# A vision tower on one core: patch loads issued by two engines in turn, and two bias products moved

## The reference

```
h = _L0_tok_ref(x, L0_tok_W, L0_tok_b)            # patches (576 x 768) @ W.T + b
h = _layernorm(h + _L0_attn_ref(h, ...))          # begins with a layer norm of h, then
                                                  # u, v, base = silu(xn @ W + b), v's bias is L0_attn_bv
```

## Time and profile before

| what | us |
|---|---|
| median of 3 executions | 157.12 |
| the three | 157.12, 155.45, 157.18 |
| profiled execution | 155.55 |
| its span (first to last instruction) | 153.8 |

### The profile page before, as it was taken

How to read it: one execution, slowest core, us unless ns; L and a number is a source line. 1 busy time by engine, 2 the same in 40 slices (tenths; PEclk the granted TensorE clock), 3 DMA queues, 4 the chain that set the end, 5 groups by cost and what they waited for, 6 DMA issues and landing times.

```text
span 153.8 us, 2915 instructions
## 1 busy us (share of the span) xinstructions
PE 141.2 (92%) x1117; PEld 71.8 (47%) x1117; DVE 98.2 (64%) x300; ACT 71.6 (47%) x136; POOL 34.7 (23%) x91
## 2 busy tenths in 40 slices
PE   6999999999999999698999977999899999999970
PEld 1435365645444345164355333547354464654550
DVE  6415958755466736756677899755758468314992
ACT  3646931675647010059244202434881356458452
POOL 8703000037777100002600004300087000000000
PEclk9999999999999999999999999999999999999999
DMA  5999992000000000000002000000000000000001
GB/s 158 341 410 399 233 364 80 4 0 2 2 4 2 0 0 0 0 4 0 0 2 60 0 2 0 0 4 0 0 4 0 0 0 2 4 0 4 0 0 38
DMA packets 3716, 8.17 MB, mean 53 GB/s; under 512 B 1579, under 2 KB 1707, under 8 KB 3574
## 3 DMA queue, kind: packets, MB, share of 16 engines
q1 hardware_dynamic: 3390, 7.87, 15.2%
q10 hardware_dynamic: 312, 0.11, 0.3%
HBM read 7.61 MB, written 0.15 MB: 50 GB/s over the span
## 4 chain that ended last, share of the span: by engine, by line
PE 68%; DVE 22%; ACT 5%; issue 3%; DVEq 0%; ACTq 0%
PE ps L417 12%; PE ps L477 10%; PE ps L464 9%; PE ps L471 4%; PE ps L424 3%; DVE scores L1384 3%; DVE residual L1505 3%; PE ps L582 2%; PE ps L432 2%; PE ps L446 2%; DVE patch_sb L1497 2%; DVE scores_rest L1405 2%; ACT hidden L925 1%; PE ps L574 1%; PE ps L631 1%
## 5 line engine op out<-in xcount | busy, mean ns | idle before, releaser
L417 PE MATMUL ps<-idle_operand 128*128 128x512 bf16 x132 | 36.2, 392 | 3.2 <-DVE scores L1384 1.6
L1203 DVE TENSOR_TENSOR hidden_gated<-hidden,ps 128x576 f32<-128x576 f32 x28 | 19.7, 751 | 10.5 <-PE ps L471 10.5
L925 ACT ACTIVATE hidden<-ps,weights_sb 128x576 f32<-128x576 f32 x28 | 19.6, 738 | 9.9 <-PE ps L464 8.2
L917 ACT ACT_TABLE_LOAD x16 | 20.5, 1283 | 0.3
L417 PEld LDWEIGHTS ps<-idle_operand 128*128 128x128 bf16 x132 | 11.1, 101 | 18.1 <-issue 3.7
L905 ACT ACTIVATE squares<-ps 128x288 f32<-128x288 f32 x7 | 2.9, 411 | 29.0 <-PE ps L672 8.4
L477 PE MATMUL ps<-hidden_gated,weights_sb 128*64 128x288 f32 x112 | 16.3, 418 | 0.0
L325 POOL CAST combine_parts_T<-combine_parts_T 64x288 f32<-64x288 bf16 x3 | 1.3, 418 | 55.7 <-DVE combine_parts_T L1150 55.7
L464 PE MATMUL ps<-h,weights_sb 64*128 64x288 f32 x80 | 13.0, 436 | 0.7 <-ACT hidden L925 0.4
L1115 DVE COPY centred<-ps 128x288 f32<-128x288 f32 x7 | 3.2, 457 | 11.4 <-ACT squares L905 11.4
L477 PEld LDWEIGHTS ps<-hidden_gated,weights_sb 128*64 128x64 f32 x112 | 6.6, 135 | 7.0 <-DVE hidden_gated L1203 2.7
(11 more groups left out here) (306 smaller groups left out, 232.6 us busy)
## 6 DMA issues: line engine op xcount, KB each, us to landing
patch_sb<-patches SPq DMA_DIRECT2D x6, 288.0 KB, 5.3
weights_sb<-weights SPq DMA_DIRECT2D x1, 1108.0 KB, 9.5
weights_sb<-weights SPq DMA_DIRECT2D x1, 717.0 KB, 16.0
weights_sb<-weights SPq DMA_DIRECT2D x1, 689.0 KB, 14.7
weights_sb<-weights SPq DMA_DIRECT2D x1, 640.0 KB, 7.4
weights_sb<-weights SPq DMA_DIRECT2D x1, 512.0 KB, 12.5
weights_sb<-weights SPq DMA_DIRECT2D x1, 394.0 KB, 14.8
selectors<-sels SPq DMA_DIRECT2D x1, 384.0 KB, 12.0
```

Of the source, the lines that this page charges most:

```text
L417: mm(PS[:, bank, :], idle_in[:, 0:P], idle_in[:, :], start=True, stop=True)
L917: act.activation(warm[:, tables[0]:tables[0] + 1], warm[:, 0:1], func)
L925: act.activation(HR[:, at % RING, :, :], two(ZA if ch % 2 == 0 else ZB), func, bias=w(f"b1_{n}")[:, ch:ch + 1]).then_inc(S["act_out"], 1)
L1203: dve.tensor_tensor(HG[:, at % GRING, :, :], HR[:, at % RING, :, :], two(GATE_AT[n][ch]), ALU.mult)\
```

## The change

The diff does four things. SyncE issues patches 0, 2 and 4; ScalarE issues 1, 3 and 5, before its first wait. The two halves of patch 0 are multiplied right after the first centring and start the sum in bank YB; the row bias is added after them, when `rows_c` is 2. Of the two value bias products only the first stays in front; the second is cut into two pieces of 256 columns. One piece takes the place of two idle products in `variance(0)`, and the other that of two of the three in `spread(0)`.

```diff
             load("tok", "tok_w")
-            for k in range(IN_K):
+            for k in range(0, IN_K, 2):
                 sp.dma_start(X[:, k, :], patches[k]).then_inc(S[f"patch{k}"], 16)
...
+            def value_bias(j, a, b):
+
+                mm(PS[:, ZB + j, a * P:b * P].rearrange("p (a e) -> p a e", a=b - a), ones[:, 0:P],
+                   w("bv_row").unsqueeze(1).to_broadcast([P, b - a, P]), start=(a == 0), stop=False, skip_group_check=True)
+
             def variance(k):
 
-                idle(2, ZA)
+                if k == 0:
+                    value_bias(1, 0, 2)
+                else:
+                    idle(2, ZA)
                 pe.wait_ge(S["sq"], k + 1)
...
                 bank = MB if k == 4 else ZA
-                idle(0 if k in (1, 3, 4) else 3, bank)
+                if k == 0:
+                    value_bias(1, 2, 4)
+                    idle(1, bank)
+                else:
+                    idle(0 if k in (1, 3, 4) else 3, bank)
                 pe.wait_ge(S["rs"], k + 1)
...
             pe.wait_ge(S["tok_w"], 16)
-            for j in range(2):
-                mm(PS[:, ZB + j, :].rearrange("p (a e) -> p a e", a=4), ones[:, 0:P],
-                   w("bv_row").unsqueeze(1).to_broadcast([P, 4, P]), start=True, stop=False, skip_group_check=True)
-            pe.wait_ge(S["rows_c"], 2)
-            mm(psY, w("tok_b_row"), ones[:, :], start=True, stop=False, skip_group_check=True)
+            value_bias(0, 0, 4)
+            pe.wait_ge(S["rows_c"], 1)
             tokw = w("tok_w").rearrange("p (k d) -> p k d", k=IN_K)
             for k in range(IN_K):
                 pe.wait_ge(S[f"patch{k}"], 16)
+                if k == 1:
+                    pe.wait_ge(S["rows_c"], 2)
+                    mm(psY, w("tok_b_row"), ones[:, :], start=False, stop=False, skip_group_check=True)
                 for h in range(2):
                     last = mm(PS[rows(h), YB, 0:HALF], tokw[:, k, :], X[:, k, h * HALF:(h + 1) * HALF],
-                              start=False, stop=(k == IN_K - 1), skip_group_check=True)
+                              start=(k == 0), stop=(k == IN_K - 1), skip_group_check=True)
...
+            for k in range(1, IN_K, 2):
+                act.dma_start(X[:, k, :], patches[k]).then_inc(S[f"patch{k}"], 16)
             act.wait_ge(S["tok_w"], 16)
```

## The result

| | before | changed |
|---|---|---|
| median of 22 executions each, us | 156.02 | 157.61 |
| lowest and highest | 155.08, 157.42 | 155.84, 159.28 |
| profiled execution, span | 155.55, 153.8 | 157.07, 155.2 |

A forecast was written before the change was run, and what follows sets the result against it. The prediction took one TensorE chain, waiting at the start for patch loads limited by DMA bytes, as the bound. Its terms came to +0.25 us on the profiled 155.55; against the mean 156.3 it gave 156.6, range 155.0 to 157.8.

The forecast's parts named there:

- Bytes, not issue, limit the patches: Patch loads at the start: SyncE issues 630 GB/s while the DMA engines move 306 to 383.
- D can come earlier only by a fuller start: Last patch's landing: a fuller third microsecond gains 0 to 0.35 us; 0.15 taken, so 9.25.
- rival A: Patch loads: two queues keep the DMA engines fuller, priced at -0.7 us, 155.6; chance 0.27.
- What stands first in SyncE's queue: First weights, sharing with patch 1, land up to 0.5 us later; what follows stays under 10 us.
- I cost it at nothing: TensorE's front: patch 0 could start 1.3 us sooner, but later DMA waits keep this off the path; 0.
- The order of arrival (+0.29): Patches 2 and 4 arrive behind later ones, TensorE waits at both, and products end at 10.44 us.
- Rival B, the clock: TensorE's clock falls in waits around the patches and products run at half speed: +3.3 us, 159.6; chance 0.06.
- the forecast's +0.25: Whole kernel: arrival order eats the fuller start, so the change is slower by 0.25 us; chance 0.50.
- TensorE's order at nothing: Patch 0's products ahead of the row bias and one value bias out of the front: 0 us.
- The bias in the norm at nothing: Second value bias, in place of idle products in the first norm, hides behind ScalarE's work: 0 us.
- the sum: Whole kernel: 155.55 us plus 0.25 gives 155.8; the first part gains at most 0.35 by the skill's rule.

The follow-up runs named there:

- e1: Kernel before with only the patch issuing changed, SyncE and ScalarE in turn, TensorE's order as before; ratio 1.0141.
- e7: Kernel before, all loads on SyncE, with patch 0 issued ahead of the first weights; ratio 1.0098.
- e10: Changed kernel with the first weight group also split between SyncE and ScalarE; ratio 1.0000.
- e13: Kernel before with three idle products at the start instead of six, loads untouched; ratio 1.0121.
- e6: Changed kernel with nine idle products at the start instead of six; ratio 1.0017.
- e12: Changed kernel with the first weights shared by both queues and eight idle products at the start; ratio 0.9994.
- e16: Changed kernel with its own loads, eleven idle products at the start and both value biases inside the first norm; ratio 1.0010.
- e0_before_marks: Kernel before with only two marks added that show when the key transfers of the second attention land; ratio 1.0001.
- e2: Kernel before with only TensorE's order changed, SyncE still issuing all six patches; ratio 0.9996.
- e5: Changed kernel with a wait ahead of ScalarE's three patch issues, which then begin at 1.86 us; ratio 1.0114.
- padded form: Kernel before with ten more idle products ahead of the wait for the key transfers; ratio 1.0116.

## Why the prediction was wrong, by its steps

- **Bytes, not issue, limit the patches: right as far as it went.** Issuing the odd patches from ScalarE brought the last issue from 3.52 to 2.1 and the last landing from 9.4 to 8.9 only, for the forecast's 9.25.
- **"D can come earlier only by a fuller start": wrong both ways.** The start was emptier (150 for 244 GB/s), and the gain came from 4 to 8 us, at 400 to 406 GB/s for 306 to 383, as rival A had it. A then needed TensorE to be ready, and it was not.
- **What stands first in SyncE's queue: the step that failed.** The forecast gave the first weights at most 0.5 us of delay, kept TensorE's start off the path even so ("I cost it at nothing", 9.5 with the delay), and did not time patch 0 again. The weights came 1.13 late (5.00 for 3.87). I estimate 0.37 of it from the third microsecond's missing 94 kB and the fourth's 48, at 383 GB/s, and the rest is the sharing with patch 1, which landed at 5.2. Patch 0 came 1.7 late (6.29 for about 4.6). So TensorE's start became the bound: centring to 6.14, patch 0 from 6.42, row bias, then five patches without a stop to 10.39. Patch 0 and the row bias also took 0.64 and 0.68 from start to next start, where the forecast had 0.49 each.
- **The order of arrival (+0.29): it came as forecast, its waits did not.** Patch 2 landed at 8.0 and patch 4 last, at 8.9, for the forecast's 8.15 and 9.25. By its own sum, with the measured 8.9, the products would have ended at 8.9 + 0.98 + 0.21 = 10.1. But TensorE came to them too late to wait: its one wait on a patch was for patch 0. That the square at 10.43 falls on the forecast's 10.44 is luck.
- **Rival B, the clock: the right mechanism, at 0.06 the wrong chance.** Its price was 3.3, the runs show 2.2 (12.67 for 10.43). It was argued away with a wait of 1.6 us later in the kernel, at a time when the clock had long been up. Here it had not yet risen: the six idle products were its run-up, and the gap came right behind them. It makes the loss at the start larger than the forecast's +0.25: with the fast bias the square was 0.23 late, with the slow one 1.45 to 2.63. Of eight profiles with 0.5 us of standing or more ahead of the value bias (the changed kernel four times, e1, e7, e10, e13), six had a slow bias, with the square at 11.65 to 12.83, and two a fast one, both at 10.43. The average loss of 0.7% is then a mixture of these. This is inferred, since only profiled executions show which kind they are; e6, e12 and e16, which bridge the gap and still issue from both engines, support it with 1.0017, 0.9994 and 1.0010. Standing is not the only thing at work: e0_before_marks had a slow bias without it.
- **TensorE's order at nothing: right** (e2, 0.9996), for as long as the clock is up. **The bias in the norm at nothing:** it was 0.09 us (3.65 for 3.56), too little for the ratios to tell.
- **The two rules of the Trainium skill.** The one cited for rival B ("TensorE: Matmul & The Clock Gate", section "HAM oscillation — how this bites in real kernels") says that waits on DMAs between bursts of products can halve the clock. Something near it happened: in e7 and e13 the products behind such a wait ran at half rate. But the idle products ahead of the wait stepped by 0.43 and were at the lower level already, so these runs show a rise that came late and not a fall. The one cited for the sum ("DMA: Bandwidth & Descriptors", section "Issuing engines are not separate DMA queues") says that several issuing engines save only issue time. Here more was moved between 4 and 6 us as well: 400 GB/s for 306 in the two profiles of the timed pair, at least 395 in every profile of the changed kernel and 304 to 365 with one queue. When ScalarE began 1.1 us later (e5), it was 310.
- **Open: the key landing.** No step of the forecast has it, though in the profiled execution it is 1.1 of the 1.4 us. That it has two values in both kernels is shown. Whether ScalarE's earlier issues make the late one likelier (seven of eleven against two of six) is not.

## What to carry to other kernels

Ask of every transfer that is moved up which transfer ahead of it now gets less of the engines, and what stands behind that one: the first weights and the first patch mattered more here than the last patch. Idle products at the start may be lost if the next work does not follow them at once (six of the eight profiles with a gap of 0.5 to 1.6 us); when that work slips, lengthen them to meet it (e6 took back most of the loss with three more). When a trace's granted clock reads 1.00, still compare the durations of equal products early and late.

## What the runs showed of the hardware

- The granted clock of the records read 1.00 in stretches where equal f32 products took twice as long (bias records 2.04 and 1.10, a patch 1.23 and 0.71).
- The same start shows the clock rising at different times: in the kernel before and its padded form the four bias records took 1.95, 2.16, 2.57 and 3.55 us in four profiles.
- With both queues in use from 0.7 us on and the first weights on SyncE's, 136 to 164 GB/s were moved between 2 and 3 us, against 214 to 254 with one queue (218 or 219 with the weights shared). Between 4 and 6 us it was 395 to 410, against 304 to 310 with one queue (364 and 365 in two profiles).
- A second queue that started 1.1 us later was served late: median landing 7.5 us against 5.7 (e5, one profile).
- Six small transfers from SBUF to SBUF, issued by two engines at once, complete either 5.0 to 5.1 or 5.8 to 6.7 us behind the first issue, in the kernel before (4.98 and 6.21) as in the others.
